# An attention stage re-staged from pairs of query tiles to single query tiles, in a fused attention and FFN layer on 8 cores

## What is computed

```python
Q = x @ WQ.T + bQ
K = jnp.tile((x @ WK.T + bK).reshape(b, t, NG, HS), (1, 1, R, 1)).reshape(b, t, NH * HS)
V = jnp.tile((x @ WV.T + bV).reshape(b, t, NG, HS), (1, 1, R, 1)).reshape(b, t, NH * HS)
scores = jnp.where(causal, -inf, einsum('btd,bsd->bts', Q, K))
attn = softmax(scores) / sqrt(128)
x = layernorm(x + einsum('bts,bsd->btd', attn, V) @ proj)
h = silu((x @ gate_w.T) * gate_s) * ((x @ up_w.T) * up_s)
x = layernorm(x + (h @ down_w.T) * down_s)
```

## Time and profile before

| what | us |
|---|---|
| two timed runs | 2008.25 and 2149.21, median 2078.73 |
| the profiled execution, its own time | 2000.01 |
| its span on the slowest core (core 3); all cores 1970.6 to 1998.5 | 1998.5 |
| attention, first score matmul to issue of the last `x1b` store, core 3 | 511.6 to 904.8 |
| first gate matmul, core 3 | 956.3 |

### The profile page before, as it was taken

The page is one execution under the profiler, slowest core; times in us unless marked ns, Lnnn a source line. Parts: engine busy times, 40 slices in busy tenths (PEclk is TensorE's granted clock), DMA queues, the critical chain, the costliest instruction groups (busy, mean ns, idle before and its releaser), DMA issues. The chain is left out here.

```text
span 1998.5 us, 19255 instructions; the slowest of 8 cores (1970.6 to 1998.5 us)
## 1 busy us (share of the span) xinstructions
PE 1441.6 (72%) x7854; PEld 767.8 (38%) x7854; DVE 334.6 (17%) x415; ACT 168.7 (8%) x214; POOL 189.1 (9%) x198
## 2 busy tenths in 40 slices
PE   0676559964476262620899999999999599999920
PEld 0232224421133030300344444444444188888820
DVE  0000001001444343430011111111111100000035
ACT  0110001110110101010100100001000000000011
POOL 1000000001000101031011111111111000000000
PEclk9887779985688686865899999999999799999965
DMA  7644674127201313139687978878778698555067
GB/s 103 94 56 65 84 105 56 29 64 127 73 0 32 116 32 116 32 113 158 66 79 69 84 70 79 80 70 83 75 73 84 66 138 131 92 87 85 30 227 285
DMA packets 296225, 175.44 MB, mean 88 GB/s; under 512 B 201692, under 2 KB 283848, under 8 KB 291017
## 3 DMA queue, kind: packets, MB, share of 16 engines
q0 software_dynamic: 258208, 106.96, 47.4%
q1 hardware_dynamic: 37930, 67.25, 10.8%
HBM read 247.60 MB, written 29.36 MB: 139 GB/s over the span
## 5 line engine op out<-in xcount | busy, mean ns | idle before, releaser
L740 PE MATMUL gups<-x1T,gstr 128*128 128x512 bf16 x1408 | 319.8, 380 | 71.0 <-DMA x1T<-x1bd 70.5
L823 PE MATMUL dnps<-dstr,hT 128*128 128x256 bf16 x2816 | 309.4, 273 | 17.6 <-DMA dstr<-dTd 17.6
L750 PE MATMUL gups<-x1T,ustr 128*128 128x512 bf16 x1408 | 318.3, 379 | 0.0
L823 PEld LDWEIGHTS dnps<-dstr,hT 128*128 128x128 bf16 x2816 | 276.4, 98 | 51.9 <-issue 19.1
L740 PEld LDWEIGHTS gups<-x1T,gstr 128*128 128x128 bf16 x1408 | 138.0, 98 | 239.2 <-issue 74.5
L750 PEld LDWEIGHTS gups<-x1T,ustr 128*128 128x128 bf16 x1408 | 137.8, 98 | 166.1
L336 PE MATMUL kps<-xch,wk_sb 128*128 128x512 bf16 x512 | 122.0, 403 | 82.7 <-DMA xch<-xT 40.8
L765 DVE SCALAR_TENSOR_TENSOR hT<-gups,us_col,silu 128x512 bf16<-128x512 f32 x88 | 66.1, 751 | 608.2 <-PE gups L750 608.2
L472 PE MATMUL scps<-kT,qsT 128*128 128x512 bf16 x256 | 75.4, 451 | 96.5 <-DVE scores L481 91.8
L354 PE MATMUL vps<-wv_sb,xch 128*128 128x512 bf16 x512 | 114.0, 384 | 13.7 <-DMA wv_sb<-wvT 13.7
L336 PEld LDWEIGHTS kps<-xch,wk_sb 128*128 128x128 bf16 x512 | 52.1, 103 | 154.9 <-issue 101.7
(11 more groups left out here) (96 smaller groups left out, 567.2 us busy)
## 6 DMA issues: line engine op xcount, KB each, us to landing
gstr<-gTd POOLq DMA_DIRECT2D x44, 512.0 KB, 7.2
ustr<-uTd POOLq DMA_DIRECT2D x44, 512.0 KB, 9.3
dstr<-dTd POOLq DMA_DIRECT2D x8, 2816.0 KB, 22.4
xch<-xT POOLq DMA_DIRECT2D x8, 2048.0 KB, 23.7
wq4b<-wq POOLq DMA_DIRECT2D x16, 512.0 KB, 9.5
masks<-msk SPq DMA_DIRECT2D x8, 1024.0 KB, 9.6
Pq<-prj POOLq DMA_DIRECT2D x16, 512.0 KB, 5.3
xqp<-xq SPq DMA_DIRECT2D x32, 256.0 KB, 3.3
```

Of the source, the lines that this page charges most:

```text
L740: (lambda bi, tch, gsl, ct: lambda e: e.matmul(gups[:, gsl, :], gstr[bi][:, ct, :], x1T[:, ct, tch*512:(tch+1)*512], start=(ct == 0), stop ...
L750: (lambda bi, tch, usl, ct: lambda e: e.matmul(gups[:, usl, :], ustr[bi][:, ct, :], x1T[:, ct, tch*512:(tch+1)*512], start=(ct == 0), stop ...
L823: (lambda bi, ts, ps, it: lambda e: e.matmul(dnps[ps][:, 0:256], hT[:, it, ts*128:(ts+1)*128], dstr[bi][:, it, :], start=(it == 0), stop=( ...
```

## The change

The unit of work in the attention stage becomes one query tile. `plan_scores`, `plan_z`, `plan_proj` and `plan_ln1` each take a tile q. The main loop runs scores of q, then z of q - 1, then projection and first norm of q - 2. z of one tile goes in 4 blocks of 8 key tiles instead of 8 blocks of 4 key tiles for two query tiles, so a block still holds 8 transposes and 8 matmuls; its bank of `zpn` is moved out by a copy of half the width, and one copy to `zT_sb` is left per tile. Its transposes wait for the exponent of their own tile (`exp_mark[q - 1]`). The counts of matmuls, transposes, loads and stores over the whole stage are the same. The records in `Builder` (`inc_log`, `tag`) are kept in Python alone.

```diff
-                zT_sb = sB("zT_sb", [128, 4, 256], BF16)
+                zT_sb = sB("zT_sb", [128, 2, 4, 128], BF16)
-                def plan_scores(g):
+                def plan_scores(q):
-                    for q in (2 * g, 2 * g + 1):
...
+                    exp_mark[q] = exp_prev
...
-                def plan_z(g):
+                def plan_z(q):
...
-                        for j in range(4):
-                            st = blk * 4 + j
-                            for qi in range(2):
-                                B.op("tensor",
-                                     (lambda st, j, qi, atp: lambda e: e.transpose(
-                                         atp[:, (j*2+qi)*128:(j*2+qi+1)*128],
-                                         Pq[:, qi, st*128:(st+1)*128], idb_sb[:]))(st, j, qi, atp),
+                        for j in range(8):
+                            st = blk * 8 + j
+                            B.op("tensor",
+                                 (lambda st, j, sl, atp: lambda e: e.transpose(
+                                     atp[:, j*128:(j+1)*128],
+                                     Pq[:, sl, st*128:(st+1)*128], idb_sb[:]))(st, j, sl, atp),
...
                     plan_tr(0)
-                    for blk in range(1, 8):
+                    for blk in range(1, 4):
                         plan_tr(blk)
                         plan_mm(blk - 1)
-                    plan_mm(7)
-                    p_free[0] = p_free[1] = B.m("pe")
+                    plan_mm(3)
+                    p_free[sl] = B.m("pe")
...
-                pending = None
-                for g in range(4):
-                    plan_scores(g)
-                    if pending is not None:
-                        plan_proj_ln1(pending)
-                    plan_z(g)
-                    if pending is not None:
-                        plan_ln1(pending)
-                    pending = g
-                plan_proj_ln1(pending)
-                plan_ln1(pending)
+                zevac_s = [0, 0]
+                exp_mark = {}
+                plan_scores(0)
+                for q in range(1, NQT):
+                    plan_scores(q)
+                    plan_z(q - 1)
+                    if q >= 2:
+                        plan_proj(q - 2)
+                        plan_ln1(q - 2)
+                plan_z(NQT - 1)
+                plan_proj(NQT - 2)
+                plan_ln1(NQT - 2)
+                plan_proj(NQT - 1)
+                plan_ln1(NQT - 1)
```

More of the change, by code:

```diff
@@ L54, in begin, with op @@
         self.cur = []
-    def op(self, eng, fn, waits=(), incs=()):
+    def op(self, eng, fn, waits=(), incs=(), tag=None):
         own = {"vector": "ve", "scalar": "se", "gpsimd": "ge"}.get(eng)
@@ L61, in op @@
             self.cnt[s] += k
+            ln = fn.__code__.co_firstlineno if fn is not None else 0
+            self.inc_log.setdefault(s, {})[self.cnt[s]] = tag or "%s@L%d" % (eng, ln)
         self.cur.append(Op(eng, fn, waits, incs))
@@ L457, in build_program @@
                 zT_used = 0
-                def plan_scores(g):
+                def plan_scores(q):
                     nonlocal exp_prev
-                    for q in (2 * g, 2 * g + 1):
[L462 to L470, removed]
-                                B.op("tensor",
[L472 to L488, removed]
-                        B.op("vector",
[L490 to L510, removed]
@@ L512, in plan_z @@
-                def plan_z(g):
-                    nonlocal zevac
+                    sl = q % 2
+                    smk = "smk%d" % sl
+                    mmsk = B.dma("sync",
+                                 (lambda q, sl: lambda e: e.dma_start(
+                                     out=masks[:, sl, :], in_=msk[q]))(q, sl),
+                                 smk, [("ve", mask_free[sl])])
+                    for ch in range(NCH):
+                        cs = ch % 2
+                        for dqt in range(4):
+                            B.op("tensor",
+                                 (lambda q, ch, cs, dqt: lambda e: e.matmul(
+                                     scps[:, cs, :],
+                                     qsT[:, q//4, dqt, (q%4)*128:(q%4+1)*128],
+                                     kT[:, ch, dqt, :],
+                                     start=(dqt == 0), stop=(dqt == 3)))(q, ch, cs, dqt),
+                                 [("ve", sc_free[cs])] if dqt == 0 else (),
+                                 [("pe", 1)] if dqt == 3 else ())
+                        mp_sc = B.m("pe")
+                        B.op("vector",
+                             (lambda ch, cs, sl: lambda e: e.scalar_tensor_tensor(
+                                 out=scores[:, ch*512:(ch+1)*512], in0=scps[:, cs, :],
+                                 scalar=1.0, in1=masks[:, sl, ch*512:(ch+1)*512],
+                                 op0=OP.mult, op1=OP.add))(ch, cs, sl),
+                             [("pe", mp_sc), (smk, mmsk), ("se", exp_prev)],
+                             [("ve", 1)])
+                        sc_free[cs] = B.m("ve")
@@ new lines, in plan_scores @@
+                    mask_free[sl] = B.m("ve")
+                    B.op("vector",
+                         (lambda q: lambda e: e.tensor_reduce(
+                             nmax8[:, q:q+1], scores[:], axis=AX.X, op=OP.max,
+                             negate=True))(q),
+                         (), [("ve", 1)])
+                    mv_max = B.m("ve")
+                    B.op("scalar",
+                         (lambda q, sl: lambda e: e.activation(
+                             out=Pq[:, sl, :], in_=scores[:], func=AF.Exp,
+                             bias=nmax8[:, q:q+1], scale=1.0,
+                             accum_out=sum8[:, q:q+1]))(q, sl),
+                         [("ve", mv_max), ("pe", p_free[sl])], [("se", 1)])
@@ new lines, in plan_scores @@
+                    exp_prev = B.m("se")
+                    exp_mark[q] = exp_prev
+                    B.op("vector",
+                         (lambda q: lambda e: e.tensor_scalar(
+                             out=tmp8[:, q:q+1], in0=sum8[:, q:q+1], scalar1=RSQ,
+                             scalar2=None, op0=OP.mult))(q),
+                         [("se", exp_prev)], [("ve", 1)])
+                    B.op("vector",
+                         (lambda q: lambda e: e.reciprocal(
+                             rec8[:, q:q+1], tmp8[:, q:q+1]))(q),
+                         (), [("ve", 1)])
@@ L515, in plan_tr @@
+                def plan_z(q):
+                    sl = q % 2
+                    zs = q % 2
+                    exp_q = exp_mark[q]
                     def plan_tr(blk):
@@ L537, in plan_mm @@
                         bk = blk % 2
[L538 to L549, removed]
+                        for j in range(8):
+                            st = blk * 8 + j
+                            B.op("tensor",
+                                 (lambda st, bk, j, zs: lambda e: e.matmul(
+                                     zpn[:, zs, :], aT_sb[:, bk, j*128:(j+1)*128],
+                                     vv[:, st, :], start=(st == 0),
+                                     stop=(st == 31)))(st, bk, j, zs),
+                                 [("ve", max(at_ready[bk], zevac_s[zs]))]
+                                 if j == 0 else (),
+                                 [("pe", 1)] if st == 31 else ())
@@ L559, in plan_z @@
                          [("pe", mp_z)], [("ve", 1)])
                     mv_zn = B.m("ve")
-                    for tq in range(2):
+                    for dv in range(4):
+                        B.op("tensor",
+                             (lambda zs, dv: lambda e: e.transpose(
+                                 atps[zs][:, dv*128:(dv+1)*128],
+                                 zn_sb[:, zs, dv*128:(dv+1)*128], idb_sb[:]))(zs, dv),
+                             [("ve", max(mv_zn, atp_free[zs])), ("pe", zT_used)]
+                             if dv == 0 else (),
+                             [("pe", 1)] if dv == 3 else ())
@@ new lines, in plan_z, with plan_proj @@
+                    mp_zt = B.m("pe")
+                    B.op("vector",
+                         (lambda zs: lambda e: e.tensor_copy(
+                             zT_sb[:, zs, :],
+                             atps[zs][:, 0:512].rearrange("p (dv t) -> p dv t", dv=4)))(zs),
+                         [("pe", mp_zt)], [("ve", 1)])
+                    zevac_s[zs] = B.m("ve")
+                    atp_free[zs] = zevac_s[zs]
+                def plan_proj(q):
+                    nonlocal zT_used
+                    tq = q % 2
+                    sx = "sx%d" % tq
+                    zs = q % 2
+                    for dc in range(4):
+                        ps = dc % 2
+                        sxq = "sxq%d" % ps
+                        mxq = B.dma("sync",
+                                    (lambda q, dc, ps: lambda e: e.dma_start(
```

(25 more changed lines are left out.)

190 lines of the change are left out of this document (82 added, 108 removed).

## The result

The changed kernel took 2043.2 us (median of 11 runs, 2034.8 to 2049.9) against 2005.1 for the kernel before in the same sessions (median of 7 runs, 2003.9 to 2008.3): a ratio of 1.0184, 95% interval 1.0162 to 1.0206. It is slower by some 37 us, and the lower end of the interval is far from 1. In some executions of these kernels the cores of one die, or of both, show a lower granted clock and the time is some per cent longer; all medians here leave them out. The profiled execution of the changed kernel took 2040.65 us, its span is 2039.1 on core 5, the slowest.

What follows compares the result with a forecast made beforehand. It took a chain hopping between engines in the attention stage, no engine full, to bound the kernel. Seven terms made a 56.2 us turn against 50.4 per tile; with start and end, 33.0 over 2000.0 gave 2033.0, range 2010 to 2051.

Steps and rivals of the forecast that it cites:

- scores: First link of a turn: from the landed mask's first use on VectorE through the tile's scores, 9.5 us.
- exponent and reciprocal: Maximum, exponent and reciprocal after the scores; not covered, so TensorE waits through most of it: 9.1 us.
- z: One tile's z, first copy to the `zn_sb` copy: 11.2 us, taken between 8.7 at full speed and 12.3 cold.
- to the first eviction: From the `zn_sb` copy through `zT_sb` to the end of the first projection chunk: 2.5 us.
- projection: Projection of tile q - 2, its third and fourth pieces of x fetched behind the first evictions: 5.9 us.
- row sum to mask: From the norm's row sum past the stores in SyncE's queue to the next mask's issue: 10.0 us.
- mask: From a mask's issue behind the stores to its first use: 8.0 us, with 5.0 and 9.9 as ends.
- that the mask would no longer be waited for: Third rival: finer staging removes the mask wait, each of five turns losing 15.6 us: 1955 us, chance 0.04.
- That it would land as it does alone: Second rival, about no change: mask takes 5.0 us in five turns, z runs warm at 8.7: 2001 us, chance 0.10.
- the upper ends would come together: First rival, slower by over 2%: mask takes 9.9 us, z stays slow for two blocks: 2050 us, chance 0.30.
- the signs that would have shown it wrong: Masks issued before the stores, z's copies running ahead of the exponent, or later stages changing length.
- how the numbers follow: Chances for the whole kernel's time: 0.66 within 2%, 0.30 slower by over 2%, 0.04 faster by over 2%.

Runs made afterwards that it cites:

- e8: Changed kernel with each tile's two stores issued by ScalarE's DMA queue instead of SyncE's, masks keeping their place in the program: 1968.6 us, ratio 0.9782.
- e2: Kernel before, with the next group's two masks issued after the previous group's pieces of x, ahead of z and the stores: 1977.1 us, ratio 0.9858.
- e1: Changed kernel with each mask issued a turn earlier, right after planning the previous tile's scores: 1967.6 us, ratio 0.9821.
- e3: Changed kernel with row-sum scaling and reciprocal moved from the end of a tile's scores to the head of its projection: 2014.4 us, ratio 1.0039.
- e4: Changed kernel with 40 unread matmuls per tile (20 for the last) added before the first z matmul: 2033.0 us, ratio 1.0132.
- e7: e6 with the last two tiles' projections planned ahead of their norms: 1911.6 us, ratio 0.9520 to the kernel before.
- e6: Changed kernel with the edits of e1 and e3 together, plus 20 unread matmuls per tile before z: 1920.6 us, ratio 0.9564.

## Why the prediction was right, and where it was wrong

The direction, the place and the size of the loss were right in the sum. It said 33.0 us for the stage (its own end, 937.5 less 904.8, is 32.7), and the stage grew by 33.3; the stated 2033.0 and the measured 2043.2 differ by what the base differs (2000.0 for the execution the sum was made against, 2005.1 for the median) and by some 4 us outside the stage, which the sum left at nothing.

Step by step, on the profile of the changed kernel: scores 688.68 - 679.22 = 9.5 (said 9.5); exponent and reciprocal 697.80 - 688.68 = 9.1 (9.1); z from 10.4 to 11.8 over the tiles, 11.8 in the turn above (11.2); to the first eviction 712.11 - 709.59 = 2.5 (2.5); projection 718.07 - 712.11 = 6.0 (5.9); row sum to mask 728.09 - 718.07 = 10.0 (10.0); mask 736.24 - 728.09 = 8.1 and 679.22 - 671.43 = 7.8 (8.0). Four turns from tile 3's first eviction at 623.22 to tile 7's at 848.72 took 56.4 each (56.2). Two of these terms, z and the mask, were picked between two ends that the rows could not tell apart (8.7 and 12.3, 5.0 and 9.9); that both came out within 0.2 of the mean is in part luck. The masks' idling is 78.1 (78), and the last store is 428 us behind the first score matmul (426). Of the signs that would have shown it wrong none appeared.

The rivals: that the mask would no longer be waited for (1955) fell with the five waits. That it would land as it does alone fell with landings of 7.3 to 7.6 on core 5. That the upper ends would come together stayed short: z was slow in every tile, but the mask took 8, not 9.9. By the fit of the Trainium skill ("DMA: Bandwidth & Descriptors", "Anatomy of one DMA") the estimate for that link was 7.2; 7.3 to 7.6 were measured. By the rule of its section "Queues, rings and completion order" the mask's completion was to come behind the stores' writes. That this sets the time is not shown: in e8, with no store just ahead of it, a mask took 7.0 (below).

What was wrong is the last step, "how the numbers follow", where the sum was turned into chances. It took 2% for "about what a measurement of this kernel can tell from no change, 40 us", a size that the text works out from no row, and so put 0.66 on "within 2%", where a loss of 33 us and no change at all stand side by side, and 0.30 on slower. The runs showed a measurement ten times as sharp: the interval is 0.2% to each side, the times of the two kernels (2003.9 to 2008.3 and 2034.8 to 2049.9) do not touch, and 1.84% stands clear of 1 as a loss. The text forecast a slower kernel in its sum and gave most of its chance to what reads as no change. A forecast of 1.65% deserved to be stated as slower, with the 2% line named as a line that the value lay next to.

Why the change lost is thus shown, by undoing one link at a time. In the loop of single tiles every mask from tile 3 on stands behind the stores of another tile's norm, in a queue that waits for GpSimd, where in the pairs one such wait served two masks. On average of the cores VectorE's idling for masks went from 42.7 to 79.1, 36.4 more, and the stage lost 33.3. Early masks win 39.1 in the staging by pairs (e2) and 77.5 in that by single tiles (e1); with them single tiles are 5.1 ahead (350.6 and 355.7), without them 33.3 behind. So the masks' place is the whole loss. The exposed exponent and the slow clock are real links of the chain (e3, e4), but they don't make single tiles slower than pairs once the masks are out of the way: the prediction counted the slow z as a cost that the pair did not pay, and what the pairs pay in its place no run took apart.

## What to carry to other kernels

A load that needs nothing stands still behind a store that waits, if both use one in-order queue: before a loop is re-staged, write down that queue's order for one turn and ask of each load which wait stands ahead of it. When work is cut finer, count how often a turn goes through the longest detour between engines; here halving the unit took it from two to five, and moving the load ahead, or the stores to another queue, took it to none. In this serial chain every link that was shortened showed nearly in full (e3 to e7), and the chain could be summed from the rows of the kernel before. How sharp a measurement is should be read from repeated runs before a forecast is turned into chances.

## What the runs showed of the hardware that was not expected

- Matmuls that nobody reads paid here. 40 of them in a wait of 10 us, 300 in all, took 15.5 us off the stage, and 160 in waits of 5.5 us took 14.5 off (e4, e6). After both lengths of idling, 10.0 and 5.5, the next eight z matmuls had taken 3.2 to 3.6 instead of 1.89.
- After the same 10.0 us of idling z took from 10.4 to 11.8 on core 5 of the changed kernel: the first eight matmuls were always slow, the next eight took from 1.89 to 2.66.
- What stands ahead of a mask changed its landing little. Behind 1.5 MB of stores (changed kernel) and behind two pieces of x with the stores elsewhere (e8) it took:

```profile
DMA to landing us min/median/max: 7.6/7.6/7.6
```

```profile
DMA to landing us min/median/max: 7.0/7.0/7.0
```

  (the masks issued at 671.43 and at 691.92, on cores 5 and 4). Over all cores the masks of tiles 3 to 7 took 7.3 to 8.4 in the changed kernel, but for one of 9.8, and 6.4 to 8.2 in e8. Alone one had taken 4.8. Which of the other transfers makes the difference was not tried.
